# Attention probabilities turned in 32 by 32 blocks on VectorE and put together by DMA, in a gated cross-attention block

## The chip, the cores and the metric

The kernel runs on one core of a Trainium2 chip. A core has TensorE (matrix products, here also transposes), VectorE, ScalarE, GpSimd and SyncE (SP), which issues DMAs in the order of its own list; sixteen DMA engines move the data. The metric is the device time in microseconds (us), median of several runs. The engines run their own instruction lists and wait for each other by semaphores.

## The reference

The block adds gated cross-attention to `x`, and then a gated, quantized feed-forward network:

```python
# x (4, 512, 1024), ctx (4, 64, 1024); 32 heads of 128, 8 KV heads (each serves 4 heads)
def xattn(q, k, v, Wq, Wk, Wv, Wd):
    queries = rope(heads(q @ Wq.T)); keys = rope(heads(k @ Wk.T)); values = heads(v @ Wv.T)
    scores = einsum('bhqd,bhkd->bhqk', queries, repeat(keys, 4)) * 128 ** -0.5
    scores = where(causal, scores, lowest)
    attn = softmax(scores, axis=-1)                 # 512 queries x 64 keys per head
    return einsum('bhqk,bhkd->bhqd', attn, repeat(values, 4)) -> rows @ Wd.T

x = x + tanh(g_xattn[0]) * xattn(layernorm(x), ctx, ctx, Wq, Wk, Wv, Wd)
x = x + tanh(g_ffn[0]) * ffn(layernorm(x), ...)     # int8-like weights and rounded activations
```

## The kernel before

The four batch elements are done in two halves of two. In each half there are 32 *units*; a unit is a pair of heads with one batch element of the half (512 queries, 64 keys, two heads: 8 blocks of 64 columns, `prob`, 128 partitions x 512). Four units, two pairs of heads by two batch elements, make a *group*, which shares one KV head. Each engine has a hand-written list, `slot(half, u)`, by the kind of the slot, `u % 4`; kind 0 begins a group. Slot u computes the queries of unit u (eight steps `queries(unit, part)`, each of two times three matmuls, since every float32 product is made of a high and a low half), the scores of unit u - 1, and the turning of the probabilities of unit u - 2, and it carries the sixteen output steps of the group before (`outputs(gg - 1, c)`, six matmuls each, 3, 5, 5 and 3 of them in kinds 0 to 3). Eight values steps (`values(gg, i)`, three matmuls: values times a piece of the output weights) are spread over kinds 2, 3 and the next 0. Outputs steps 0 to 7 read the turned probabilities of the group's units 0 and 2, steps 8 to 15 those of units 1 and 3. `last_outputs` does the rest of the last group of a half.

The way of a unit's probabilities: VectorE does the mask, maximum and subtraction (`softmax_a`), ScalarE the exponential, VectorE the sum, the reciprocal and the product (`softmax_b`). TensorE then turns four blocks of 128 x 128 into a PSUM bank (`turn_probs`, line 544), ScalarE copies them rounded to `pt_hi` (line 837), VectorE subtracts to get `pt_lo` (`lower_probs`, line 1112 by `lower`), and the output steps read both. ScalarE's copy waits until the output steps of the group before have read the buffer (`o_ps`).

The lists are in order, so an instruction that waits holds back all behind it. In kind 3 ScalarE's list is: split weights 8g+3, copy values 2, split 8g+4, split a query weight, copy values 3, split 8g+5, `copy_probs`, split a query weight, split 8g+6, exponential, copy values 4 and 5. VectorE's: `turn_second` (rotation), adds 13 to 15 with values 2 and 3 lowered between them, `lower_probs`, `softmax_a`, `turn_first`, values 4, `softmax_b`, values 5. The first queries step of a slot waits for the `turn_first` of the unit before. An output step c waits until VectorE has added step c - 2 (two PSUM banks).

SP issues the loads: query weights `wq_raw` (four DMAs for each pair of heads), output weights `wd_raw` (a ring of three, `WDS`; load v + 3 is issued by `next_wd(v)` once values step v has run, line 341), keys `kblk`, values `v_t`. Its list waits too.

Of the kernel before, what the change touches and what calls it, by code (L numbers as in the profile page):

```python
# [91 lines left out]
def gated_block(nc, x, ctx_t, g_att, g_ffn, wq_t, wk_t, wv_t, wd_t, wg_t, wu_t, wo_t,  # L92
# [6 lines left out]
    with root:  # L99
# [3 lines left out]
        def sb(stack, name, shape, dt):  # L103
            return stack.enter_context(nc.sbuf_tensor(name, [P] + shape, dt))
# [32 lines left out]
        with ExitStack() as s:  # L137
            pt_hi = sb(s, "pt_hi", [2, HB, CH], F32R)
            pt_lo = sb(s, "pt_lo", [2, HB, CH], F32R)
# [20 lines left out]
            acc = sb(s, "acc", [HTILES, DIM], F32)  # L160

# [56 lines left out]
        pt_ps, pt_hi_done, pt_lo_done = sem("pt_ps"), sem("pt_hi_done"), sem("pt_lo_done")  # L218
# [19 lines left out]
        Q_BANK, S_BANK, T_BANK, O_BANK, V_BANK = 0, 2, 3, 4, 6  # L238
        scores, p_turned = bank(S_BANK), bank(T_BANK)
# [34 lines left out]
        def _(sp):  # L274
# [83 lines left out]

            load_k(0)
            load_v(0)  # L360
            for half in range(HALVES):
                for u in range(UNITS):
                    unit, gg = half * UNITS + u, half * GROUPS + u // UPG
                    if u % 2 == 0 and unit // 2 + 1 < HALVES * PAIRS and unit != UNITS:
                        if unit >= 2:
                            sp.wait_ge(q_done, unit)
                        load_wq(unit // 2 + 1)
# [13 lines left out]
                    if u % UPG == 3:  # L381
                        for i in range(2, 6):
                            next_wd(VPG * gg + i)
                    if u == 3 and half == 1:
                        for t in range(HTILES):
                            sp.wait_ge(x1_store[t], 16)
                            sp.wait_ge(part_done, TILES + t + 1)
                            sp.dma_start(acc[:, t, :], x[HTILES + t, :, :]).then_inc(x_in[t], 16)
                if half == 0:
# [11 lines left out]
                    load_v(GROUPS)  # L401
                    sp.wait_ge(xt_ps, HTILES + 1)
# [6 lines left out]
            sp.wait_ge(q_done, HALVES * UNITS)  # L409

# [41 lines left out]
        def _(pe):  # L452
# [86 lines left out]
            def turn_probs(unit):  # L539
                pe.wait_ge(p_done, unit + 1)  # L540
                if unit:
                    pe.wait_ge(pt_lo_done, unit)
                for t in range(BT):
                    ins = pe.transpose(p_turned[:, t * P:(t + 1) * P], prob[:, 2 * t:2 * t + 2, :].rearrange("p a b -> p (a b)"), ident)  # L544
                ins.then_inc(pt_ps, 1)

# [28 lines left out]
            def slot(half, u):  # L575
                unit, gg, kind, filled = half * UNITS + u, half * GROUPS + u // UPG, u % UPG, u >= UPG
                queries(unit, 0)
                if kind == 0:
                    if filled:
                        turn_probs(unit - 2)  # L580
# [26 lines left out]
                if kind == 1:  # L607
                    if filled:
                        turn_probs(unit - 2)
                        outputs(gg - 1, 3)  # L610
# [16 lines left out]
                if kind == 2:  # L627
                    turn_probs(unit - 2)
# [20 lines left out]
                if kind == 3:  # L649
# [10 lines left out]
                    turn_probs(unit - 2)  # L660
# [9 lines left out]
            def last_outputs(half):  # L670
                unit, gg = (half + 1) * UNITS, (half + 1) * GROUPS
                turn_probs(unit - 2)
# [10 lines left out]
                turn_probs(unit - 1)  # L683
# [86 lines left out]
        def _(act):  # L770
# [61 lines left out]
            def copy_probs(unit):  # L832
                p, b, gg = (unit // HB) % 2, unit % HB, unit // UPG
                act.wait_ge(pt_ps, unit + 1)
                if gg >= 1:
                    act.wait_ge(o_ps, (gg - 1) * OPG + (b + 1) * 2 * BT)
                act.activation(pt_hi[:, p, b, :], p_turned, ACT.Copy).then_inc(pt_hi_done, 1)  # L837
# [270 lines left out]
        def _(dve):  # L1108
# [122 lines left out]
            def softmax_a(unit):  # L1231
# [9 lines left out]
                if unit:  # L1241
                    dve.wait_ge(pt_ps, unit)
# [3 lines left out]
            def softmax_b(unit):  # L1246
# [8 lines left out]
                                  ALU.mult).then_inc(p_done, 1)  # L1255

            def lower_probs(unit):
                p, b = (unit // HB) % 2, unit % HB
                dve.wait_ge(pt_hi_done, unit + 1)
                lower(pt_lo[:, p, b, :], p_turned, pt_hi[:, p, b, :], pt_lo_done)  # L1260
# [268 lines left out]
```

## Time and profile before

| | |
|---|---|
| median of 3 runs | 1,588.74 us (1,587.85 to 1,589.26) |
| the profiled execution | 1,585.7 us, its span 1,583.9 us |
| granted TensorE clock, mean | 0.983 |
| busy: TensorE, VectorE, ScalarE, GpSimd | 94%, 63%, 34%, 38% |
| DMA queue q1 | 197,536 packets, 138.67 MB, 30.8% of 16 engines' span |

A row of the costliest groups reads: line, engine, operation, output <- inputs, count | busy us, mean ns of one | idle of the engine just before them and what ended it. Timeline rows start with the start and the duration in us; matmuls overlap, so the distance between two starts is what one costs. A row on SPq gives the time for which an issue held SP.

### The profile page before, as it was taken

What the parts mean: (1) busy time and instruction counts of PE and PEld (TensorE: products, weight loads), DVE (VectorE), ACT (ScalarE), POOL (GpSimd) and SP (SyncE); (2) the same over time, 40 slices, a digit from 0 to 9 for tenths busy, and PEclk for the clock granted to TensorE, in tenths of its full rate; (3) what the DMA queues carried; (4) which work ended last, traced back from release to release, by engine and by line L of the source; (5) the groups of instructions that cost most, each with busy time, mean ns of one, the idle gap of its engine ahead of it and who ended that gap; (6) DMA issues with size and microseconds to landing.
All of it is one profiled execution on the core that took longest, in us unless ns stands there. A gap on an engine that the chain in (4) does not pass through costs nothing.

```text
span 1583.9 us, 19344 instructions
## 1 busy us (share of the span) xinstructions
PE 1490.7 (94%) x7507; PEld 1223.5 (77%) x7520; DVE 993.9 (63%) x1562; ACT 539.1 (34%) x832; POOL 603.8 (38%) x392
## 2 busy tenths in 40 slices
PE   6879999999999999998898999999999999976996
PEld 5858888888888888886777888888888888854553
DVE  5747565656565656666474656565656565668995
ACT  3323232323232323244242313232323232317884
POOL 0044333343434333330333333333333434214996
PEclk9999999999999999999999999999999999998999
DMA  8723222221222222227233222222222211192553
GB/s 268 229 49 84 65 61 68 58 68 57 68 56 69 60 65 62 65 61 242 52 146 75 64 52 60 53 59 55 58 55 56 55 56 46 37 282 85 195 178 141
DMA packets 198058, 143.05 MB, mean 90 GB/s; under 512 B 147152, under 2 KB 167760, under 8 KB 197584
## 3 DMA queue, kind: packets, MB, share of 16 engines
q1 hardware_dynamic: 197536, 138.67, 30.8%
q0 software_dynamic: 432, 3.15, 0.9%
q8 instruction: 60, 0.98, 0.3%
q14 instruction: 30, 0.25, 0.1%
HBM read 125.01 MB, written 19.92 MB: 92 GB/s over the span
## 4 chain that ended last, share of the span: by engine, by line
PE 80%; DVE 8%; ACT 4%; POOL 3%; issue 2%; DMA 1%; SPq 1%; POOLq 0%; DVEq 0%; ACTq 0%
PE psum L455 16%; PE psum L457 16%; PE psum L456 16%; PE psum L535 7%; PE psum L570 7%; PE psum L572 7%; PE psum L571 7%; POOL go L1084 2%; PE psum L544 2%; DVE stat L1150 1%; DVE sc L1422 1%; ACT xg L973 1%; DMA kv_w<-in_wk_t 1%; ACT xu L974 1%; PE psum L502 1%
## 5 line engine op out<-in xcount | busy, mean ns | idle before, releaser
L455 PE MATMUL psum<-xt_hi,wq_hi 128*128 128x512 f32 x1024 | 407.0, 397 | 13.3 <-DVE rot L1220 8.6
L457 PE MATMUL psum<-xt_hi,wq_lo 128*128 128x512 f32 x1024 | 401.0, 392 | 0.0
L456 PE MATMUL psum<-xt_lo,wq_hi 128*128 128x512 f32 x1024 | 400.6, 391 | 0.0
L1028 POOL TENSOR_TENSOR rot<-rot 128x1024 f32<-128x1024 f32 x64 | 153.4, 2397 | 467.7 <-DVE rot L1228 465.8
L1276 DVE TENSOR_TENSOR acc<-psum,acc 128x512 f32<-128x512 f32 x256 | 175.7, 688 | 164.2 <-PE psum L572 162.1
L1007 POOL TENSOR_TENSOR wd_lo<-wd_raw,wd_hi 128x512 fp32r<-128x512 f32 x128 | 164.1, 1288 | 227.6 <-ACT wd_hi L795 227.6
L1007 POOL TENSOR_TENSOR wq_lo<-wq_raw,wq_hi 128x512 fp32r<-128x512 f32 x128 | 162.7, 1286 | 202.6 <-ACT wq_hi L790 202.6
L455 PEld LDWEIGHTS psum<-xt_hi,wq_hi 128*128 128x128 f32 x1024 | 193.6, 189 | 53.1 <-issue 5.2
L1112 DVE TENSOR_TENSOR vw_lo<-psum,vw_hi 64x512 fp32r<-64x512 f32 x256 | 176.2, 689 | 81.1 <-ACT vw_hi L848 75.3
L457 PEld LDWEIGHTS psum<-xt_hi,wq_lo 128*128 128x128 f32 x1024 | 193.4, 189 | 41.2
L456 PEld LDWEIGHTS psum<-xt_lo,wq_hi 128*128 128x128 f32 x1024 | 193.9, 189 | 38.6
L848 ACT ACTIVATE vw_hi<-psum 64x512 fp32r<-64x512 f32 x256 | 151.3, 591 | 210.3 <-PE psum L457 207.2
L570 PE MATMUL psum<-vw_hi,pt_hi 128*128 128x512 f32 x512 | 206.7, 404 | 6.5 <-DVE pt_lo L1112 4.3
L572 PE MATMUL psum<-vw_hi,pt_lo 128*128 128x512 f32 x512 | 200.5, 392 | 0.0
L571 PE MATMUL psum<-vw_lo,pt_hi 128*128 128x512 f32 x512 | 200.4, 391 | 0.0
L837 ACT ACTIVATE pt_hi<-psum 128x512 fp32r<-128x512 f32 x64 | 38.3, 598 | 303.0 <-PE psum L544 303.0
L852 ACT ACTIVATE prob<-prob 128x512 f32<-128x512 f32 x64 | 40.3, 630 | 285.1 <-DVE prob L1243 285.1
L535 PEld LDWEIGHTS psum<-kblk,rot 128*128 128x128 f32 x1024 | 126.6, 195 | 10.3 <-issue 5.2
L1235 DVE TENSOR_TENSOR psum<-psum,cst 128x128 f32<-128x128 f32 x64 | 19.2, 299 | 180.6 <-PE psum L535 180.6
L535 PE MATMUL psum<-kblk,rot 128*128 128x128 f32 x1024 | 127.2, 278 | 4.4 <-POOL rot L1028 4.4
L570 PEld LDWEIGHTS psum<-vw_hi,pt_hi 128*128 128x128 f32 x512 | 96.9, 189 | 28.1 <-DVE pt_lo L1112 5.7
L572 PEld LDWEIGHTS psum<-vw_hi,pt_lo 128*128 128x128 f32 x512 | 96.5, 189 | 20.7
(118 smaller groups left out, 1961.1 us busy)
## 6 DMA issues: line engine op xcount, KB each, us to landing
wq_raw<-in_wq_t SPq DMA_DIRECT2D x128, 256.0 KB, 4.5
wd_raw<-in_wd_t SPq DMA_DIRECT2D x128, 256.0 KB, 3.0
acc<-in_x SPq DMA_DIRECT2D x16, 512.0 KB, 8.1
x_scratch<-acc SPq DMA_DIRECT2D x16, 512.0 KB, 7.4
xa<-x_scratch SPq DMA_DIRECT2D x16, 512.0 KB, 3.3
xb<-x_scratch SPq DMA_DIRECT2D x16, 512.0 KB, 4.3
xn<-in_x SPq DMA_DIRECT2D x10, 512.0 KB, 4.3
kv_w<-in_wk_t SPq DMA_DIRECT2D x4, 1024.0 KB, 8.5
```

The lines of the kernel that those rows point to most:

```text
L455: pe.matmul(dst, a_hi, b_hi, start=start, stop=False)
L456: pe.matmul(dst, a_hi, b_lo, start=False, stop=False)
L457: return pe.matmul(dst, a_lo, b_hi, start=False, stop=stop)
L535: ins = pe.matmul(scores[:, t * P:(t + 1) * P], rot[:, 0, j, t * P:(t + 1) * P], kblk[:, j, 2 * b:2 * b + 2, :].rearrange("p a k -> p (a k ...
L570: pe.matmul(dst, p_hi, vw_hi[:, p, b, cols], start=(p == 0), stop=False)
L571: pe.matmul(dst, p_hi, vw_lo[:, p, b, cols], start=False, stop=False)
L572: ins = pe.matmul(dst, p_lo, vw_hi[:, p, b, cols], start=False, stop=(p == 1))
L848: act.activation(vw_hi[rows, p, bl, cols], bank(V_BANK + i % 2)[rows, :], ACT.Copy).then_inc(vw_hi_done, 1)
L1007: pool.tensor_tensor(dst, full, hi.bitcast(F32), ALU.subtract).then_inc(done, 1)
L1028: pool.tensor_tensor(rot[:, 0, :, :], rot[:, 0, :, :], rot[:, 1, :, :], ALU.add).then_inc(rope_done, 1)
L1112: dve.tensor_tensor(dst, full, hi.bitcast(F32), ALU.subtract).then_inc(done, 1)
L1276: dve.tensor_tensor(acc[:, tile, cols], bank(O_BANK + c % 2), acc[:, tile, cols], ALU.add).then_inc(o_done, 1)
```

## The change

`turn_probs` is gone from TensorE's list, and its PSUM bank is unused. At the end of `softmax_b` VectorE turns `prob` in 32 by 32 blocks into a new buffer `turned`. SP then puts each block in its place with sixteen DMAs of 32 partitions x 4 x 32 elements (`move_probs`), from quadrant a to quadrant c, into `pt_raw`, which shares its memory with `pt_lo`. ScalarE rounds `pt_raw` to `pt_hi` and VectorE lowers `pt_raw` in place. The wait for the output steps of the group before moves from ScalarE to SP.

```diff
         with ExitStack() as s:
             pt_hi = sb(s, "pt_hi", [2, HB, CH], F32R)
+            with ExitStack() as over:
+                pt_raw = sb(over, "pt_raw", [2, HB, CH], F32)
             pt_lo = sb(s, "pt_lo", [2, HB, CH], F32R)
...
+            turned = sb(s, "turned", [BT, 4, 32], F32)
...
+            def move_probs(unit):
+                p, b, gg = (unit // HB) % 2, unit % HB, unit // UPG
+                if gg >= 1:
+                    sp.wait_ge(o_ps, (gg - 1) * OPG + (b + 1) * 2 * BT)
+                sp.wait_ge(turned_done, unit + 1)
+                dst = pt_raw[:, p, b, :].rearrange("q (t a i) -> q t a i", a=4, i=32)
+                for a in range(4):
+                    for c in range(4):
+                        sp.dma_start(dst[32 * c:32 * c + 32, :, a, :], turned[32 * a:32 * a + 32, :, c, :]).then_inc(pt_in[unit % 2], 16)
...
                     unit, gg = half * UNITS + u, half * GROUPS + u // UPG
+                    if u % UPG == 3:
+                        move_probs(unit - 2)
                     if u % 2 == 0 and unit // 2 + 1 < HALVES * PAIRS and unit != UNITS:
...
                         for i in range(2, 6):
                             next_wd(VPG * gg + i)
+                    if u % UPG != 2 and u >= 1:
+                        move_probs(unit - 1)
...
+                    move_probs(UNITS - 1)
...
+            move_probs(HALVES * UNITS - 1)
...
-            def turn_probs(unit):
-                pe.wait_ge(p_done, unit + 1)
-                if unit:
-                    pe.wait_ge(pt_lo_done, unit)
-                for t in range(BT):
-                    ins = pe.transpose(p_turned[:, t * P:(t + 1) * P], prob[:, 2 * t:2 * t + 2, :].rearrange("p a b -> p (a b)"), ident)
-                ins.then_inc(pt_ps, 1)
...
             def copy_probs(unit):
-                p, b, gg = (unit // HB) % 2, unit % HB, unit // UPG
-                act.wait_ge(pt_ps, unit + 1)
-                if gg >= 1:
-                    act.wait_ge(o_ps, (gg - 1) * OPG + (b + 1) * 2 * BT)
-                act.activation(pt_hi[:, p, b, :], p_turned, ACT.Copy).then_inc(pt_hi_done, 1)
+                p, b = (unit // HB) % 2, unit % HB
+                act.wait_ge(pt_in[unit % 2], 256 * (unit // 2 + 1))
+                act.activation(pt_hi[:, p, b, :], pt_raw[:, p, b, :], ACT.Copy).then_inc(pt_hi_done, 1)
...
-                if unit:
-                    dve.wait_ge(pt_ps, unit)
...
                                   ALU.mult).then_inc(p_done, 1)
+                dve.wait_ge(p_done, unit + 1)
+                if unit:
+                    dve.wait_ge(pt_in[(unit - 1) % 2], 256 * ((unit - 1) // 2 + 1))
+                dve.transpose(turned[:, :, :, :], prob[:, :, :].rearrange("p (t h) (m k) -> p t (h m) k", t=BT, k=32)).then_inc(turned_done, 1)
...
-                lower(pt_lo[:, p, b, :], p_turned, pt_hi[:, p, b, :], pt_lo_done)
+                lower(pt_lo[:, p, b, :], pt_raw[:, p, b, :], pt_hi[:, p, b, :], pt_lo_done)
```

SP's list from kind 2 of one group to the key load in kind 0 of the next, before the change; a row is a DMA, what it waits for and how many alike follow:

```order
L300 DMA wq_raw<-in_wq_t 128x8x64 [waits q_done]
L300 DMA wq_raw<-in_wq_t 128x8x64 x3
L306 DMA wd_raw<-in_wd_t 128x512 [waits vw_ps] x6
L300 DMA wq_raw<-in_wq_t 128x8x64 [waits q_done]
L300 DMA wq_raw<-in_wq_t 128x8x64 x3
L306 DMA wd_raw<-in_wd_t 128x512 [waits vw_ps]
L336 DMA kblk<-kv_scratch 64x2x64 [waits s_done]
```

The same place after it, with the move that kind 1 leaves ahead of it:

```order
L372 DMA pt_raw<-turned 32x4x32 [waits turned_done,o_ps]
L372 DMA pt_raw<-turned 32x4x32 x15
L304 DMA wq_raw<-in_wq_t 128x8x64 [waits q_done]
L304 DMA wq_raw<-in_wq_t 128x8x64 x3
L310 DMA wd_raw<-in_wd_t 128x512 [waits vw_ps] x2
L372 DMA pt_raw<-turned 32x4x32 [waits turned_done,o_ps]
L372 DMA pt_raw<-turned 32x4x32 x15
L310 DMA wd_raw<-in_wd_t 128x512 [waits vw_ps] x4
L372 DMA pt_raw<-turned 32x4x32 [waits turned_done,o_ps]
L372 DMA pt_raw<-turned 32x4x32 x15
L304 DMA wq_raw<-in_wq_t 128x8x64 [waits q_done]
L304 DMA wq_raw<-in_wq_t 128x8x64 x3
```

The six loads of output weights in a row are now two and four, with a move between them, and each query weight load stands behind a move.

VectorE's list in kind 3, from the lower half of the probabilities to values 5, before:

```order
L1112 TENSOR_TENSOR pt_lo<-psum,pt_hi 128x512 [waits pt_hi_done]
L1235 TENSOR_TENSOR psum<-psum,cst 128x128 [waits s_done]
L1239 TENSOR_REDUCE red<-psum 128x8 [waits mask_done]
L1243 TENSOR_TENSOR prob<-psum,red 128x512 [waits pt_ps,max_done]
L1220 TENSOR_TENSOR rot<-psum,cst 128x1024 [waits s_done,qa_done]
L1112 TENSOR_TENSOR vw_lo<-psum,vw_hi 64x512 [waits vw_hi_done] x2
L1248 TENSOR_REDUCE red<-prob 128x8 [waits exp_done]
L1250 RECIPROCAL red<-red 128x8 [waits sum_done]
L1252 TENSOR_SCALAR red<-red,gates 128x8 [waits rcp_done]
L1254 TENSOR_TENSOR prob<-prob,red 128x512 [waits share_done]
L1112 TENSOR_TENSOR vw_lo<-psum,vw_hi 64x512 [waits vw_hi_done] x2
```

And after:

```order
L1116 TENSOR_TENSOR pt_lo<-pt_raw,pt_hi 128x512 [waits pt_hi_done]
L1239 TENSOR_TENSOR psum<-psum,cst 128x128 [waits s_done]
L1243 TENSOR_REDUCE red<-psum 128x8 [waits mask_done]
L1245 TENSOR_TENSOR prob<-psum,red 128x512 [waits max_done]
L1224 TENSOR_TENSOR rot<-psum,cst 128x1024 [waits s_done,qa_done]
L1116 TENSOR_TENSOR vw_lo<-psum,vw_hi 64x512 [waits vw_hi_done] x2
L1250 TENSOR_REDUCE red<-prob 128x8 [waits exp_done]
L1252 RECIPROCAL red<-red 128x8 [waits sum_done]
L1254 TENSOR_SCALAR red<-red,gates 128x8 [waits rcp_done]
L1256 TENSOR_TENSOR prob<-prob,red 128x512 [waits share_done]
L1261 STREAM_TRANSPOSE turned<-prob 128x512 [waits pt_in1,p_done]
L1116 TENSOR_TENSOR vw_lo<-psum,vw_hi 64x512 [waits vw_hi_done] x2
```

One instruction is added behind the product, with a wait for the moves of the unit before; the subtraction no longer waits for TensorE's turn.

## Rows read from the trace of the kernel before

**Rows 1.** The page's busy times: us, share of the span, instructions.

```profile
PE 1490.7 (94%) x7507; PEld 1223.5 (77%) x7520; DVE 993.9 (63%) x1562; ACT 539.1 (34%) x832; POOL 603.8 (38%) x392
```

**Rows 2.** The page's chain that ended last, by engine.

```profile
PE 80%; DVE 8%; ACT 4%; POOL 3%; issue 2%; DMA 1%; SPq 1%; POOLq 0%; DVEq 0%; ACTq 0%
```

**Rows 3.** Windows, one steady group: length, busy per engine, clock, DMA share, GB/s.

```profile
401.32:481.17 79.85, 79.85 (x393) 67.28 (x392) 48.51 (x74) 22.43 (x40) 29.80 (x20) 1.00 0.26 64
```

**Rows 4.** Timeline of TensorE in kind 3, from the slot's first queries step.

```profile
373.39 0.39 PE L455 MATMUL psum<-xt_hi,wq_hi 128*128 128x512 f32 x1
...
374.75 0.39 PE L570 MATMUL psum<-vw_hi,pt_hi 128*128 128x512 f32 x1
...
376.11 0.39 PE L455 MATMUL psum<-wd_hi,v_t 128*128 128x512 f32 x1
...
382.91 0.60 PE L544 MATMUL psum<-cst,prob 128*128 128x128 f32 x4
...
384.05 0.39 PE L455 MATMUL psum<-xt_hi,wq_hi 128*128 128x512 f32 x1
...
384.75 1.95 PE L535 MATMUL psum<-kblk,rot 128*128 128x128 f32 x16
386.45 0.48 PE L455 MATMUL psum<-xt_hi,wq_hi 128*128 128x512 f32 x1
...
391.30 0.39 PE L455 MATMUL psum<-wd_hi,v_t 128*128 128x512 f32 x1
```

**Rows 5.** Timeline of VectorE in the same slot: mask, rotation, sum, product.

```profile
386.73 0.30 DVE L1235 TENSOR_TENSOR psum<-psum,cst 128x128 f32<-128x128 f32 x1 [1.86 <-PE psum L535]
...
388.40 1.21 DVE L1220 TENSOR_TENSOR rot<-psum,cst 128x1024 f32<-128x1024 f32 x1
...
391.10 0.69 DVE L1248 TENSOR_REDUCE red<-prob 128x8 f32<-128x512 f32 x1
...
392.32 0.69 DVE L1254 TENSOR_TENSOR prob<-prob,red 128x512 f32<-128x512 f32 x1
```

**Rows 6.** The page's costliest groups: output weights lowered, values copied, probabilities copied.

```profile
L1007 POOL TENSOR_TENSOR wd_lo<-wd_raw,wd_hi 128x512 fp32r<-128x512 f32 x128 | 164.1, 1288 | 227.6 <-ACT wd_hi L795 227.6
...
L848 ACT ACTIVATE vw_hi<-psum 64x512 fp32r<-64x512 f32 x256 | 151.3, 591 | 210.3 <-PE psum L457 207.2
...
L837 ACT ACTIVATE pt_hi<-psum 128x512 fp32r<-128x512 f32 x64 | 38.3, 598 | 303.0 <-PE psum L544 303.0
```

**Rows 7.** Three lines' DMA issues: SP held (ns min/median/max), us from issue to landing.

```profile
L336 SPq DMA_DIRECT2D kblk<-kv_scratch x64: 584/606/1343, 78.9 to 1316.2; - x64
...
DMA to landing us min/median/max: 2.0/2.2/4.3
...
L306 SPq DMA_DIRECT2D wd_raw<-in_wd_t x128: 327/333/1717, 58.5 to 1379.6; - x128
...
DMA to landing us min/median/max: 2.9/3.0/5.6
...
L300 SPq DMA_DIRECT2D wq_raw<-in_wq_t x128: 545/674/8558, 49.7 to 1306.7; - x128
```

**Rows 8.** Timeline of SP's queue: four issues in a row, twice.

```profile
393.54 3.15 SPq L300 DMA_DIRECT2D wq_raw<-in_wq_t  x4
...
403.29 2.55 SPq L336 DMA_DIRECT2D kblk<-kv_scratch  x4
```

**Rows 9.** Windows and timeline of TensorE after an idle at the half's end.

```profile
720.00:722.00 2.00, 1.51 (x4) 1.22 (x5) 0.00 (x0) 0.00 (x0) 0.44 (x1) 0.50 0.76 217
...
720.49 0.80 PE L455 MATMUL psum<-wd_hi,v_t 128*128 128x512 f32 x1 [3.12 <-POOL wd_lo L1007]
...
723.22 0.46 PE L570 MATMUL psum<-vw_hi,pt_hi 128*128 128x512 f32 x1
```

**Rows 10.** Timeline of TensorE in the last outputs of half 1: steps 0 and 8.

```profile
1386.16 0.51 PE L570 MATMUL psum<-vw_hi,pt_hi 128*128 128x512 f32 x1 [0.71 <-DVE pt_lo L1112]
...
1407.98 0.50 PE L570 MATMUL psum<-vw_hi,pt_hi 128*128 128x512 f32 x1 [1.41 <-DVE pt_lo L1112]
```

More of the change, by code:

```diff
@@ L217, in gated_block @@
         sum_done, rcp_done, share_done, p_done = sem("sum_done"), sem("rcp_done"), sem("share_done"), sem("p_done")
-        pt_ps, pt_hi_done, pt_lo_done = sem("pt_ps"), sem("pt_hi_done"), sem("pt_lo_done")
+        turned_done, pt_hi_done, pt_lo_done = sem("turned_done"), sem("pt_hi_done"), sem("pt_lo_done")
+        pt_in = [sem("pt_in0"), sem("pt_in1")]
         vw_ps, vw_hi_done, vw_lo_done = sem("vw_ps"), sem("vw_hi_done"), sem("vw_lo_done")
@@ L235, in gated_block @@
         out_store = [sem(f"out_store{k}") for k in range(4)]
-        Q_BANK, S_BANK, T_BANK, O_BANK, V_BANK = 0, 2, 3, 4, 6
-        scores, p_turned = bank(S_BANK), bank(T_BANK)
+        Q_BANK, S_BANK, O_BANK, V_BANK = 0, 2, 4, 6
+        scores = bank(S_BANK)
         def turn_banks(half, t):
@@ L578, in slot @@
                 if kind == 0:
-                    if filled:
-                        turn_probs(unit - 2)
                     queries(unit, 1)
@@ L608, in slot @@
                     if filled:
-                        turn_probs(unit - 2)
                         outputs(gg - 1, 3)
@@ L627, in slot @@
                 if kind == 2:
-                    turn_probs(unit - 2)
                     if filled:
@@ L659, in slot @@
                         outputs(gg - 1, 15)
-                    turn_probs(unit - 2)
                     queries(unit, 3)
@@ L671, in last_outputs @@
                 unit, gg = (half + 1) * UNITS, (half + 1) * GROUPS
-                turn_probs(unit - 2)
                 values(gg - 1, 6)
@@ L682, in last_outputs @@
                     outputs(gg - 1, c)
-                turn_probs(unit - 1)
                 if half == 0:
```

## The prediction

> **What bounds the kernel now.** I read the page first, for which engine is busy; then the chain of waits; then one steady group by windows; then the timelines of TensorE, VectorE and SP for one slot. TensorE is busy 94% of the span and VectorE 63% [rows 1], and the chain that ended last lies 80% on TensorE [rows 2]. In a steady group (four slots, one KV head) TensorE is busy all 79.85 us and VectorE 48.5 [rows 3]. So for most of the span TensorE's list of matmuls is the time: whatever leaves it is won, and whatever makes it wait is lost. Against that stands a queue which nobody waits for today: SP, which issues the DMAs.
>
> One step (6 matmuls) of queries or outputs takes 1.36 us of TensorE, a values step, three matmuls, half of that, a score 1.8 (1.70 and a slower first matmul behind it) [rows 4]. With 8 query steps in each slot, 3, 5, 5 and 3 output steps in kinds 0 to 3, 2, 0, 2 and 4 values steps and one score, the slots take 18.1, 19.5, 20.8 and 19.5 us: 78.0 us, and four turns make 79.85.
>
> **What leaves.** Four transposes per unit: from 382.91 to 384.05 the turn and three matmuls take 1.14 us, where three matmuls take 0.68 [rows 4], so a turn costs 0.46 us; 64 of them are 29.5 us. This is the whole gain on TensorE.
>
> **What comes, per unit.** VectorE turns 128x512 values in blocks. No such instruction is in the trace; its other passes over 128x512 take 0.69 us [rows 5], a ScalarE pass 0.60 [rows 6]; one over twice the columns 1.21 [rows 5], which I take as the slow end, and 0.60 as the fast one. I take 0.7, the row over the same tile. It also moves the release of the move behind the probabilities. VectorE has 31 us idle per group, so its busy time costs nothing; its place in the chain below does. ScalarE's copy (0.6) and VectorE's lower half (0.7) stay, now out of SBUF; nothing speaks for another duration.
>
> Sixteen DMAs on SP, each 32 partitions x 4 runs of 128 bytes. SBUF to SBUF is not in the trace. Bounds of one issue: the 128x512 weight loads wd_raw hold SP 0.33 us, the kblk loads 0.61 (four take 2.55, so one each 0.64), the wq_raw loads 0.67 (four in 3.15, one each 0.79) [rows 7, 8]. The kblk load is nearest: also a part of the partitions, and 128 short runs or fewer. I take 0.64: 16 hold SP for 10.2 us. The last lands 2.2 us after its issue (kblk; wd_raw 3.0), so **a move takes 15 x 0.64 + 2.2 = 11.8 us** from its release. It can't come out below 2.2, the landing of a single one.
>
> The Trainium skill (DMA: Bandwidth & Descriptors, section Anatomy of one DMA) puts the sequencer's dispatch at about 50 ns and nearly all of a DMA's fixed 2 us in the receipt. By that sixteen would land 3 us after release, and the sum would come to some 1,610 us. The landing agrees with rows 7; the 0.33 to 0.79 us for which one issue holds SP do not, and the measurement decides.
>
> **Where it lies on the path.** Times from the start of a kind 3 slot of group g (373.39 in the trace), with no turns.
> Kind 3: the move of unit 4g+1 overwrites what outputs step 15 reads, so it waits for it: 9.5. Issues run to 19.7, the last lands at 21.3. Behind them in SP's queue is the load of weights 8g+5 (lands 3.0 later, 22.8), which until now was issued before step 15. ScalarE splits it (0.6), GpSimd lowers it (1.3 [rows 6]): 24.8. TensorE wants it for values step 5 at 17.4 (391.30 less 373.39 and a turn): **7.4 us of waiting**. ScalarE's copy of the probabilities stands behind that split (24.0), VectorE's lower half ends at 24.7, and behind it stand the first part of the softmax (1.85 with its gaps: from 386.73 to just past the rotation's start at 388.40 [rows 5]), and the rotation (1.2), which releases the next slot's queries: 27.8, another 1.0. Exponential (0.6), values copy (two of 0.6 [rows 6]), values lower (two of 0.7), second part of the softmax (1.95 from 391.10 [rows 5]) and the new turn then end at about 32.1.
> Kind 0 (starts 27.8): the move of unit 4g+2 lands at 43.9, copy and lower end at 45.4. Outputs step 0 wants it after 4.8 us of slot, at 32.6: **12.8 us**. Its score ends at 50.1, the turned probabilities of 4g+3 are there at 57.4 (behind a values lower of 1.4 and the rotation).
> Kind 1 (58.9): that move lands at 69.2; copy, lower and output add 3 end at 71.4, outputs step 5 wants the bank at 68.9: **2.5 us**.
> Kind 2 (81.0): the move of 4g+4 waits for outputs step 7 and its turn, 78.6; lands 90.4; copy, lower and add 8 end at 92.6; outputs step 10 wants that at 87.8: **4.8 us**. The slot ends at 106.7.
> So a group takes 106.7 us and not 79.85: **+26.8**, the turns' gain counted in.
>
> The clock: after 3.1 us of idle, from 720.49 to 723.22 a matmul took 0.6 us or more and the granted clock was 0.50, the 1.2 GHz level [rows 9]; six matmuls in 2.73 us instead of 1.36, so some 1.3 us lost. At the end of the second half an idle of 1.4 us before 1408 was followed by full speed [rows 10]. Of the four waits, the one of kind 3 is covered by that of kind 0; kind 0 would pay 2 and kind 2 1: +3 per group.
>
> **The sum**, against the profiled run (1,585.7 us, span 1,583.9): 14 full groups x (26.8 + 3) = 417. The two ends of a half: from the last slot's end to outputs step 8 took 22 us (from step 0 at 1386.2 to step 8 at 1408.0 [rows 10]); now, from the last slot's end at 27.8, step 0 waits to 45.4 as above, the score ends at 50.8, its probabilities are turned 5.4 later, and with 11.8 + 1.4 step 8 starts at 69.5: 42 us instead of 22, and 2 for the clock, 44 for both halves. The first group of a half has no outputs, but VectorE stands behind the copies: 7.5 each, 15. 1,585.7 + 417 + 44 + 15 = 2,062. The median shown is 3 us above this run: **about 2,062 us stays my number**, the 3 being less than any rounding here.
>
> **Bounds.** With 0.36 us per issue a move takes 7.6 us and holds SP 5.8: waits of 3 + 1, 8.6, 0 and 0.7 per group, 11.4 net, with a clock share of 1.5: 14 x 12.9 = 181, ends 22, first groups 10: 1,799. With 0.79: 14.05 us, each of the four stages 2.3 longer: 14 x 9.2 + 10 more, 2,200. A block turn of 1.21 adds 0.5 at three places a group, 21 us. Bytes: 131,072 more packets; the trace's average is 0.308 x 16 x 1,583.9 / 197,536 = 40 ns of one engine, so 128 packets per engine in a move are 5 us, under the 10.2 of issuing.
>
> **Rivals.**
> 1. *The same waits, cheap issues* (0.33 to 0.45): 1,800 to 1,890. For it: wd_raw's rows. Against: the only load that takes part of the partitions has 0.61.
> 2. *Dear moves*: issues as wq_raw's or packets of twice the average, so that the rings bind: 2,150 to 2,250. For it: one wq_raw issue held SP 8.6 us [rows 7], behind a full queue.
> 3. *Nearly free issues* (under 0.1). A move then takes 3 us. Weights 8g+5 land at 13.4 of kind 3, in time; VectorE's softmax starts 2.4 late behind the copies, the turned probabilities are there at 22.7, the move, copy and lower end at 27.1, and outputs step 0 wants them at 24.3: 2.8 us of waiting against 1.9 of gain, 14 x 0.9 and some 12 at the ends, 1,610. Against: the shortest issue in rows 7 is 0.33. The Trainium skill's dispatch figure, named above, would end here.
> 4. *Faster*: the moves hide and only the turns' gain stays, 1,585.7 - 29.5 = 1,556. The softmax's end (393.0) lies 19.6 us into kind 3, outputs step 0 at 19.95 + 4.8 + 0.5 = 25.2 [rows 4, 5]: 5.6 us; less the block turn 0.7 and copy and lower 1.4, 3.5 are left for a move. With a landing of 2.2 the other fifteen issues may take 1.3 us, under 0.09 each: it turns there, and only if kind 3 doesn't slip as in rival 3.
>
> **Chances.** My forecast, issues near 0.6 (1,930 to 2,150): 0.62, time 2,062; rival 1 0.17; rival 2 0.16; rival 3 0.02; rival 4 0.02; 0.01 for a sum of gain and waits that comes to nothing. Faster and slower count from 0.2%, about what a measurement of this kernel can tell: faster 0.02, same 0.01, slower 0.97. The range takes rivals 1 and 2 nearly whole: 1,800 to 2,210.
>
> **What the next profile would show.** Right: the move's DMA issues near 0.6 us each, 1,024 of them; ScalarE's pt_hi waiting for those DMAs in every slot; TensorE idle before outputs step 0 (some 13 us) and before values step 5 (some 7); a group near 107 to 110 us; the granted clock well under 1.00 at the middle of the span. Wrong: TensorE still busy through a steady group, or its waits ending on VectorE's passes with the DMAs long landed. If the issues take 0.6 and the group is not near 107, the path above is wrong; if they don't, only their size.

## The result, and the profile after

| | before | after |
|---|---|---|
| median | 1,588.3 us (1,585.66 to 1,589.26, 4 runs) | 2,119.85 us (2,119.3 to 2,125.37, 4 runs) |
| span of the profiled execution | 1,583.9 us | 2,118.2 us |
| granted TensorE clock, mean | 0.983 | 0.866 |
| a steady group (eleven, from outputs step 0 to outputs step 0) | 79.85 us | 110.1 to 114.5, mean 112.9; the one shown 113.4 |

The changed kernel takes 1.336 times as long (95% interval 1.334 to 1.3382). Forecast were 2,062 us and a range of 1,800 to 2,210: the time is 58 us above the number and inside the range. Two executions further down, one of experiment 4 (2,659 us) and one of the kernel before beside experiments 1 to 4 (2,183 us), ran at a lower clock throughout and are in no number.

The page of the changed kernel: busy times, the granted clock in 40 slices, the chain that ended last by engine; it answers to [rows 1, 2].

```profile
PE 1599.8 (76%) x7264; PEld 1282.8 (61%) x7264; DVE 1040.7 (49%) x1626; ACT 537.0 (25%) x832; POOL 609.0 (29%) x392
...
PEclk9788979798988889796988889897979897977899
...
PE 37%; SPq 29%; DVE 13%; DMA 9%; ACT 6%; issue 5%; POOL 2%; POOLq 0%; ACTq 0%; DVEq 0%
```

TensorE has 243 instructions fewer and is busy 109 us longer; it idles 518 us instead of 93. The chain, which before lay 80% on TensorE and 1% on SP's queue, now lies 29% on SP's queue and 9% on DMAs. A "busy" matmul may be a slow one: this row alone says that the clock has a part in the loss.

The costliest groups that answer to [rows 6], each with the idle time of its engine before it:

```profile
L583 PE MATMUL psum<-vw_hi,pt_hi 128*128 128x512 f32 x512 | 227.7, 445 | 292.0 <-DVE pt_lo L1116 201.3
...
L1116 DVE TENSOR_TENSOR pt_lo<-pt_raw,pt_hi 128x512 fp32r<-128x512 f32 x64 | 54.7, 855 | 664.5 <-ACT pt_hi L841 664.5
...
L841 ACT ACTIVATE pt_hi<-pt_raw 128x512 fp32r<-128x512 f32 x64 | 40.0, 625 | 741.8 <-DMA pt_raw<-turned 741.8
...
L801 ACT ACTIVATE wd_hi<-wd_raw 128x512 fp32r<-128x512 f32 x128 | 78.1, 621 | 247.1 <-DMA wd_raw<-in_wd_t 246.4
```

Read from the DMA on, that is a chain: ScalarE waits 741.8 us for moves, VectorE 664.5 us for ScalarE's copies, TensorE 201.3 us for VectorE's lower halves. The last row is the second way: ScalarE also waits 246.4 us for output weights, loads that stand behind a move in SP's list.

The steps of one move, by line (count, then min/median/max in ns):

```profile
L372 SPq DMA_DIRECT2D pt_raw<-turned x1024: 585/601/1555, 125.4 to 1937.4; - x171
...
DMA to landing us min/median/max: 1.8/1.9/6.4
...
L1261 DVE STREAM_TRANSPOSE turned<-prob x64: 711/711/716, 124.6 to 1926.5; 128x512 f32<-128x512 f32 x64
```

The block turn is 0.71 us, an issue holds SP 0.60 us, and its DMA lands 1.9 us after the issue began: forecast were 0.7, 0.64 with its spacing, and 2.2.

The timeline of SP and of the three engines behind it, in a kind 3 slot of the changed kernel and up to outputs step 0 of the next (start, duration, row, idle before and who ended it):

```profile
600.80 11.05 SPq L372 DMA_DIRECT2D pt_raw<-turned  x16
...
611.90 1.54 SPq L310 DMA_DIRECT2D wd_raw<-in_wd_t  x3
...
616.21 0.63 ACT L801 ACTIVATE wd_hi<-wd_raw 128x512 fp32r<-128x512 f32 x1 [16.92 <-DMA wd_raw<-in_wd_t]
616.75 0.61 ACT L841 ACTIVATE pt_hi<-pt_raw 128x512 fp32r<-128x512 f32 x1
616.92 1.27 POOL L1011 TENSOR_TENSOR wd_lo<-wd_raw,wd_hi 128x512 fp32r<-128x512 f32 x1 [17.76 <-ACT wd_hi L801]
...
617.39 1.34 DVE L1116 TENSOR_TENSOR pt_lo<-pt_raw,pt_hi 128x512 fp32r<-128x512 f32 x1 [15.89 <-ACT pt_hi L841]
...
618.15 1.73 POOL L1011 TENSOR_TENSOR wq_lo<-wq_raw,wq_hi 128x512 fp32r<-128x512 f32 x1
...
618.25 0.80 PE L476 MATMUL psum<-wd_hi,v_t 128*128 128x512 f32 x1 [9.55 <-POOL wd_lo L1011]
...
624.97 0.71 DVE L1261 STREAM_TRANSPOSE turned<-prob 128x512 f32<-128x512 f32 x1
...
625.77 10.54 SPq L372 DMA_DIRECT2D pt_raw<-turned  x16
...
637.55 0.63 ACT L841 ACTIVATE pt_hi<-pt_raw 128x512 fp32r<-128x512 f32 x1 [14.29 <-DMA pt_raw<-turned]
...
638.22 0.69 DVE L1116 TENSOR_TENSOR pt_lo<-pt_raw,pt_hi 128x512 fp32r<-128x512 f32 x1 [9.97 <-ACT pt_hi L841]
...
638.96 0.79 PE L583 MATMUL psum<-vw_hi,pt_hi 128*128 128x512 f32 x1 [11.37 <-DVE pt_lo L1116]
```

The rows show the forecast's chain link by link. Sixteen issues hold SP from 600.80 to 611.85. The first weight load behind them starts at 611.90 and is there at 616.2. Split, lowered by GpSimd, it frees TensorE at 618.25 (values step 5, 9.55 us of idle). VectorE's softmax is late by then; its block turn ends at 625.7, the next move holds SP from 625.77 to 636.3 and lands at 637.5, and outputs step 0 starts at 638.96, after 11.37 us of idle.

Four windows, each the 5 us of TensorE from the end of one of the four waits of a steady group, and the group itself, which answers to [rows 3] (length, busy of each engine, clock, DMA share, GB/s):

```profile
575.36:580.36 5.00, 5.00 (x18) 4.14 (x19) 1.23 (x2) 0.11 (x1) 0.00 (x0) 0.66 0.66 130
618.25:623.25 5.00, 5.00 (x12) 3.95 (x13) 4.82 (x8) 2.92 (x6) 2.87 (x2) 0.51 0.16 52
638.96:643.96 5.00, 5.00 (x13) 3.94 (x14) 1.93 (x3) 1.54 (x4) 1.27 (x1) 0.54 1.06 211
666.51:671.51 5.00, 5.00 (x15) 3.95 (x16) 4.86 (x9) 1.34 (x3) 4.22 (x4) 0.66 0.01 4
561.85:675.27 113.42, 86.69 (x377) 71.10 (x376) 51.32 (x78) 22.85 (x40) 30.10 (x20) 0.86 0.25 54
```

The group of 113.42 us is 86.69 busy and 26.73 idle. The same work at full clock is 78.0 (experiment 1 shows 77.92). So 8.7 us a group is TensorE at a lower clock; the four windows hold 5 x (0.34 + 0.49 + 0.46 + 0.34) = 8.2 of it.

### The profile page after: what moved, and what is told of

The parts are those of the page before. It is cut to its first block, busy times and chain, and to the rows that moved or that the text cites. A ratio compares the mean times of both kernels' runs of the same rounds, so it can differ in the third digit from the quotient of the medians.

```text
span 2118.2 us, 19870 instructions
## 1 busy us (share of the span) xinstructions
PE 1599.8 (76%) x7264; PEld 1282.8 (61%) x7264; DVE 1040.7 (49%) x1626; ACT 537.0 (25%) x832; POOL 609.0 (29%) x392
## 4 chain that ended last, share of the span: by engine, by line
PE 37%; SPq 29%; DVE 13%; DMA 9%; ACT 6%; issue 5%; POOL 2%; POOLq 0%; ACTq 0%; DVEq 0%
SPq L372 28%; PE psum L476 6%; PE psum L477 6%; PE psum L478 6%; PE psum L583 5%; PE psum L585 4%; PE psum L584 4%; DMA pt_raw<-turned 4%; DMA wd_raw<-in_wd_t 3%; PE psum L556 3%; DVE pt_lo L1116 2%; ACT pt_hi L841 2%; POOL go L1088 1%; DVE vw_lo L1116 1%; DVE acc L1282 1%
## 5 line engine op out<-in xcount | busy, mean ns | idle before, releaser
L583 PE MATMUL psum<-vw_hi,pt_hi 128*128 128x512 f32 x512 | 227.7, 445 | 292.0 <-DVE pt_lo L1116 201.3
L476 PE MATMUL psum<-xt_hi,wq_hi 128*128 128x512 f32 x1024 | 430.3, 420 | 14.7 <-DVE rot L1224 11.0
L477 PE MATMUL psum<-xt_lo,wq_hi 128*128 128x512 f32 x1024 | 424.0, 414 | 0.0
L478 PE MATMUL psum<-xt_hi,wq_lo 128*128 128x512 f32 x1024 | 420.2, 410 | 0.0
L1116 DVE TENSOR_TENSOR pt_lo<-pt_raw,pt_hi 128x512 fp32r<-128x512 f32 x64 | 54.7, 855 | 664.5 <-ACT pt_hi L841 664.5
L841 ACT ACTIVATE pt_hi<-pt_raw 128x512 fp32r<-128x512 f32 x64 | 40.0, 625 | 741.8 <-DMA pt_raw<-turned 741.8
L584 PE MATMUL psum<-vw_lo,pt_hi 128*128 128x512 f32 x512 | 218.6, 427 | 0.0
L585 PE MATMUL psum<-vw_hi,pt_lo 128*128 128x512 f32 x512 | 217.9, 426 | 0.0
L476 PE MATMUL psum<-wd_hi,v_t 128*128 128x512 f32 x128 | 59.4, 464 | 147.1 <-POOL wd_lo L1011 134.5
L801 ACT ACTIVATE wd_hi<-wd_raw 128x512 fp32r<-128x512 f32 x128 | 78.1, 621 | 247.1 <-DMA wd_raw<-in_wd_t 246.4
```

Source lines behind the costliest of these rows:

```text
L476: pe.matmul(dst, a_hi, b_hi, start=start, stop=False)
L477: pe.matmul(dst, a_hi, b_lo, start=False, stop=False)
L478: return pe.matmul(dst, a_lo, b_hi, start=False, stop=stop)
L583: pe.matmul(dst, p_hi, vw_hi[:, p, b, cols], start=(p == 0), stop=False)
L584: pe.matmul(dst, p_hi, vw_lo[:, p, b, cols], start=False, stop=False)
L585: ins = pe.matmul(dst, p_lo, vw_hi[:, p, b, cols], start=False, stop=(p == 1))
```

## The experiments

The kernel before ran beside each of them; ratios are to it. The theory after the result: the loss is SP's queue, held 10 to 11 us by each move, through two things that stand behind it (the move's own landing, and the weight load 8g+5), and the clock after each wait. The first rival: the landing and the exchange of the blocks by DMA cost most, and the issues little. The second: VectorE's added pass and its new order cost.

### 1. No move at all

`move_probs` and its calls are gone; ScalarE and VectorE read `turned` itself, so the blocks are not exchanged between quadrants. The wait for the output steps of the group before is ScalarE's again.

```diff
-                for a in range(4):
-                    for c in range(4):
-                        sp.dma_start(dst[32 * c:32 * c + 32, :, a, :], turned[32 * a:32 * a + 32, :, c, :]).then_inc(pt_in[unit % 2], 16)
...
-                act.wait_ge(pt_in[unit % 2], 256 * (unit // 2 + 1))
-                act.activation(pt_hi[:, p, b, :], pt_raw[:, p, b, :], ACT.Copy).then_inc(pt_hi_done, 1)
...
+                act.wait_ge(turned_done, unit + 1)
+                if gg >= 1:
+                    act.wait_ge(o_ps, (gg - 1) * OPG + (b + 1) * 2 * BT)
+                act.activation(pt_hi[:, p, b, :], turned[:, :, :, :].rearrange("q t a i -> q (t a i)"), ACT.Copy).then_inc(pt_hi_done, 1)
...
-                lower(pt_lo[:, p, b, :], pt_raw[:, p, b, :], pt_hi[:, p, b, :], pt_lo_done)
+                lower(pt_lo[:, p, b, :], turned[:, :, :, :].rearrange("q t a i -> q (t a i)"), pt_hi[:, p, b, :], pt_lo_done)
```

> The changed kernel without its moves: ScalarE and VectorE read the block-turned buffer directly (left out: the sixteen DMAs per unit, so the blocks stay in their quadrants). Theory (all of the loss is in the moves): TensorE's gain of 64 x 0.46 us alone, 1,556 to 1,562 us, no idle of TensorE in a steady group. Rival (VectorE's added pass and the longer way of the probabilities cost of themselves): above 1,588, with TensorE waiting before outputs step 0.

Measured: 1,564.0 us (1,563.23 to 1,568.08), ratio 0.9868 (0.9849 to 0.9887). Two steady groups by windows:

```profile
161.98:239.90 77.92, 77.92 (x378) 65.70 (x378) 51.00 (x78) 23.20 (x42) 30.87 (x20) 1.00 0.26 66
239.90:317.82 77.92, 77.92 (x378) 65.71 (x378) 51.01 (x78) 22.73 (x41) 30.92 (x20) 1.00 0.26 65
```

TensorE never idles in a steady group, and VectorE has its 2.5 us more per group for nothing. The second rival falls. What leaves is worth 79.85 - 77.92 = 1.93 us a group, 31 for sixteen, near the 29.5 forecast; of it 23 us are seen, and the time is 2 us above the expected interval. By the two pages TensorE idles 98.9 us of the span here and 93.2 before: the difference of 5.7 lies outside the steady groups and is most of the missing rest. The whole loss of the changed kernel against this one, 556 us, comes with the moves.

### 2 and 3. The same move as one DMA, and as four

One DMA of 128 x 512 elements, then four of 32 x 512, each from a quadrant to itself. Bytes are the same, but blocks do not change quadrants.

```diff
-                for a in range(4):
-                    for c in range(4):
-                        sp.dma_start(dst[32 * c:32 * c + 32, :, a, :], turned[32 * a:32 * a + 32, :, c, :]).then_inc(pt_in[unit % 2], 16)
+                sp.dma_start(pt_raw[:, p, b, :], turned[:, :, :, :].rearrange("q t a i -> q (t a i)")).then_inc(pt_in[unit % 2], 16)
```

> One DMA of 128 partitions x 512 per unit in place of sixteen: the same bytes (left out: the crossing of the quadrants). Theory (the price is the number of issues, 0.64 us of SP each): a move takes 2 us, the path in kind 3 does not slip and outputs step 0 is met by a hair, 1,556 to 1,570 us. Rival (any DMA between VectorE's turn and the copy costs a wait, by landing and handoffs): 1,600 or more.

> Four DMAs of 32 partitions x 512 per unit, from each quadrant to itself: the same bytes in a quarter of the issues (left out: the crossing of the quadrants). Theory (number of issues): a move takes 3 x 0.64 + 1.9 = 3.8 us and holds SP 2.6; waits of 1.6 in kind 3 and 4.8 in kind 0, less 1.9 of gain, with the clock about 5.8 per group, 14 groups and the ends: 1,670 to 1,690 us. Rival (bytes or packets bind): close to 2,118, or as the one-DMA version with no difference between the two.

Measured: with one DMA 1,670.67 us, ratio 1.0542 (1.0516 to 1.0569), a group 83.1 to 86.2 us; with four 1,709.54 us, ratio 1.0779 (1.0762 to 1.0796), a group 85.0 to 88.9 us. With 4 issues a group instead of 64, 449 us leave the changed kernel. Both runs also leave out the crossing of the quadrants and move runs of 2 KB where the sixteen have 128 bytes. But the small DMAs land no later (1.9 us after their issue, the one of 256 KB 2.4), and in the changed kernel fifteen issues of 0.60 us make most of a move's length. So the number of issues is the main cost. Between 4 and 16 issues, one more per unit is worth (2,119.85 - 1,709.54) / 12 = 34 us, 2.1 us a group. The first rival falls in the main, but not whole: both runs came out slower than expected, by 101 and 20 us, and the one with one DMA lies where its rival had it, above 1,600. A DMA that lands 2.4 us after its release should nearly have been hidden. Its timeline shows why it isn't:

```profile
481.43 0.50 SPq L370 DMA_DIRECT2D pt_raw<-turned  x1
...
485.77 0.63 ACT L799 ACTIVATE wd_hi<-wd_raw 128x512 fp32r<-128x512 f32 x1 [5.84 <-DMA wd_raw<-in_wd_t]
486.31 0.62 ACT L839 ACTIVATE pt_hi<-pt_raw 128x512 fp32r<-128x512 f32 x1
486.48 1.29 POOL L1009 TENSOR_TENSOR wd_lo<-wd_raw,wd_hi 128x512 fp32r<-128x512 f32 x1 [6.66 <-ACT wd_hi L799]
486.95 1.36 DVE L1114 TENSOR_TENSOR pt_lo<-pt_raw,pt_hi 128x512 fp32r<-128x512 f32 x1 [4.83 <-ACT pt_hi L839]
...
497.91 2.34 POOL L1030 TENSOR_TENSOR rot<-rot 128x1024 f32<-128x1024 f32 x1 [7.19 <-DVE rot L1230]
498.43 2.37 DVE L1114 TENSOR_TENSOR pt_lo<-pt_raw,pt_hi 128x512 fp32r<-128x512 f32 x1 [0.60 <-ACT pt_hi L839]
...
500.85 0.80 PE L581 MATMUL psum<-vw_hi,pt_hi 128*128 128x512 f32 x1 [4.64 <-DVE pt_lo L1114]
```

Two things. The move waits in SP's list until the outputs of the group before have read the buffer, the load behind it with it, and ScalarE's copy of the probabilities, which landed at 484.96, stands behind the split of that load at 485.77: all of VectorE's softmax slips. The block turn of unit 4g+2 ends 1.0 us before TensorE is ready for outputs step 0; in experiment 1 it is 4.3 us. And the lower half, 0.69 us before, takes 1.36 and 2.37 us while GpSimd runs. Four DMAs show the same two waits:

```profile
494.64 0.50 PE L475 MATMUL psum<-wd_hi,v_t 128*128 128x512 f32 x1 [2.05 <-POOL wd_lo L1010]
...
507.67 0.79 PE L582 MATMUL psum<-vw_hi,pt_hi 128*128 128x512 f32 x1 [4.32 <-DVE pt_lo L1115]
```

### 4. The changed kernel, with two weight loads ahead of the kind 3 move

```diff
-                    if u % UPG == 3:
-                        move_probs(unit - 2)
...
                     if u % UPG == 3:
-                        for i in range(2, 6):
-                            next_wd(VPG * gg + i)
+                        next_wd(VPG * gg + 2)
+                        next_wd(VPG * gg + 3)
+                        move_probs(unit - 2)
+                        next_wd(VPG * gg + 4)
+                        next_wd(VPG * gg + 5)
```

> The changed kernel with one edit in SP's list of kind 3: the output weight loads behind values steps 2 and 3 are issued ahead of the move of unit 4g+1. It takes away TensorE's wait before values step 5 (9.5 us a group in the changed kernel). Theory (that wait is covered: the same move also holds VectorE's softmax and the next slot's first queries): only 2 to 2.5 us a group come back, 2,080 to 2,095 us, and TensorE now waits some 6 us at the first queries step of kind 0. Rival (the waits add up): 14 x 9.5 less, about 1,985 us.

Measured: 2,066.19 us (2,063.3 to 2,067.98, 3 runs), ratio 1.3023 (1.3 to 1.3047), 54 us under the changed kernel. The wait before values step 5 took 8.4 to 10.1 us in each of 14 groups, 128 us; taking away what makes it returns 54. So more than half of it is covered, as this theory had it, and the rival (the waits add up) falls. That with the softmax earlier the move for outputs step 0 is still the late one, and that TensorE now waits at the first queries step of kind 0, is argued, not shown. The time is 14 us below the expected interval: 3.8 us a group come back, of which one spell of low clock less may be a part (2.45 us in the window above). That share is not shown either.

### 5. One DMA and the loads first

Both edits together.

> The one-DMA version (quadrants not crossed) with the two output weight loads of kind 3 issued ahead of the move. Theory (what the one-DMA version paid was its place in SP's list: the load issued behind the move landed 3.8 us later, ScalarE's split of it stands ahead of the copy, and the softmax slipped by 2.4; the rest is VectorE's lower half, 1.4 to 2.4 us where both inputs are in SBUF and GpSimd is busy): the slip goes, a wait of 1 to 2 us in kind 0 stays, 1,580 to 1,605 us. Rival (landing and handoffs alone make the 84 us above the unmoved version): no more than 10 us come back, 1,660.

Measured: 1,615.89 us, ratio 1.0189 (1.0174 to 1.0205), 55 us under experiment 2, a group 79.8 to 83.3 us. The loads' place in SP's list is worth as much with one DMA as with sixteen. The rival (no more than 10 us come back) falls. The expectation missed by 11 us, and what stays is 1.6 to 3.5 us of idle in each steady group and the two ends:

```profile
484.05 0.72 PE L582 MATMUL psum<-vw_hi,pt_hi 128*128 128x512 f32 x1 [2.52 <-DVE pt_lo L1115]
```

This is outputs step 0, behind the unit whose softmax ends last: even a move of one DMA does not fit between it and its reader. Rival 4 of the prediction had 3.5 us left there after block turn, copy and lower; a DMA that lands 2.4 us after its release and a lower half that takes up to 2.2 us longer fill more than that (2.38 us for the half, 1.7 more than alone, in the group of this row).

### 6. All sixteen DMAs, their readers as late as they may be

The order of ScalarE's copies and VectorE's lower halves becomes units 0, 2, 1, 3 of a group. Units 0 and 1 are copied a slot later, in kind 3 and at the end of kind 0; unit 3 is copied later within kind 1; units 1 and 3, which are read from outputs step 8 on, now stand behind an exponential. SP issues query weights and two output weights ahead of the moves. It does the whole computation.

```diff
+        def place(unit):
+
+            return UPG * (unit // UPG) + (0, 2, 1, 3)[unit % UPG] + 1
...
                     split_wd(VPG * gg + 5)
-                    copy_probs(unit - 2)
+                    copy_probs(unit - 3)
```

> All sixteen DMAs for all units, complete computation. Units 4g, 4g+1 and 4g+3 are copied and lowered later than in the changed kernel (kind 3, the end of kind 0 and the end of kind 1), still ahead of the output steps that read them; SP issues loads ahead of moves where it can. Only unit 4g+2 keeps its tight place. Theory (the loss is latency at four places, of which three have slack in the lists): the waits of kinds 1, 2 and 3 go, in kind 0 some 10 us stay, 1,740 to 1,800 us. Rival (SP's 41 us of issuing per group, or VectorE and GpSimd hindering each other, set the pace whatever the order): above 1,950.

Measured: 1,797.42 us (1,796.17 to 1,801.59), ratio 1.1332 (1.1316 to 1.1347): 322 us under the changed kernel with the same 1,024 DMAs. A steady group by windows, its only wait, and VectorE's block turn of unit 4g+2 ahead of it:

```profile
359.99:451.94 91.95, 80.44 (x378) 67.30 (x378) 51.62 (x78) 23.21 (x42) 30.27 (x21) 0.93 0.30 67
...
432.98 0.71 DVE L1269 STREAM_TRANSPOSE turned<-prob 128x512 f32<-128x512 f32 x1 [3.04 <-DMA pt_raw<-turned]
...
446.69 0.80 PE L590 MATMUL psum<-vw_hi,pt_hi 128*128 128x512 f32 x1 [11.51 <-DVE pt_lo L1124]
```

91.95 - 80.44 is that wait, 11.5 us, the same as the changed kernel has at this place (11.37). Three of the four waits were the order's. This one is the move of unit 4g+2, 13.0 us from the end of its block turn (433.69) to its reader, with 1.5 us of cover. Without moves the cover is 4.3 us (experiment 1). It is less here because the turn itself waits 3.04 us for the DMAs of unit 4g+1, now late, to leave the one buffer `turned`; it does so in every group, by 2.1 to 3.2 us. So a part of this wait is the buffer's; a second `turned` was not tried, and neither were issues from a second engine's queue. And with one wait the clock costs 80.44 - 77.92 = 2.5 us.

### 7 and 8. A version for this wait

In 7, unit 4g+2 of each group is turned by TensorE as before the change and the other 48 by blocks, in the order of experiment 6. In 8, the last unit of each half too: 18 on TensorE and 46 by blocks. Both do the whole computation. The first lines are experiment 8's, the last ones stand in experiment 7.

```diff
+        def on_pe(unit):
+
+            return unit % UPG == 2 or unit % UNITS == UNITS - 1
...
                 if kind == 0:
+                    if filled:
+                        turn_probs(unit - 2)
```

> As the late version, but unit 4g+2 is turned on TensorE as in the kernel before; the other 48 units go by VectorE and DMAs. Complete computation. Theory (a move costs nothing where the lists leave it 12 us and more): TensorE wins 48 turns; the version without moves showed 23 us for 64, so 17 us: 1,567 to 1,574 us, faster than both kernels. Rival (the added SP and VectorE work costs something even off the path): 1,585 or more.

> The hybrid with the last unit of each half turned on TensorE too (18 units on TensorE, 46 by VectorE and DMAs), complete computation. The hybrid's steady group took 78.41 us against 79.85, which is 14 x 1.44 = 20 us won, and its trace shows the loss at the ends of the halves: waits of 6.3 and 9.6 us before outputs step 8, with the slow clock behind them. Theory (those two moves, released in the last outputs with 5 output steps of cover, ate the gain): they go, 1,569 to 1,577 us. Rival (the loss at the ends is elsewhere, in the row loads and x rows that SP issues there): above 1,583.

Measured: experiment 7 took 1,592.33 us (5 runs), ratio 1.0037 (1.0024 to 1.0049), a miss of 18 us that lies where its rival had it, above 1,585; experiment 8 took 1,575.93 us (1,573.8 to 1,576.88, 5 runs) beside 1,586.32 of the kernel before, ratio 0.993 (0.9916 to 0.9943). In experiment 7 the groups are right, 78.4 us, and the two ends lose; its rows before outputs step 8 of the last group of each half:

```profile
737.06 0.79 PE L606 MATMUL psum<-vw_hi,pt_hi 128*128 128x512 f32 x1 [6.31 <-DVE pt_lo L1148]
...
1411.39 0.79 PE L606 MATMUL psum<-vw_hi,pt_hi 128*128 128x512 f32 x1 [9.56 <-DVE pt_lo L1148]
```

The same two places in experiment 8, and a steady group of it:

```profile
733.72 0.50 PE L612 MATMUL psum<-vw_hi,pt_hi 128*128 128x512 f32 x1 [0.54 <-DVE pt_lo L1155]
...
1399.42 0.50 PE L612 MATMUL psum<-vw_hi,pt_hi 128*128 128x512 f32 x1 [1.41 <-DVE pt_lo L1155]
...
321.40:399.80 78.40, 78.40 (x381) 66.09 (x381) 50.82 (x78) 22.96 (x41) 30.23 (x20) 1.00 0.34 74
```

The group is 78.40 us, 1.45 under [rows 3]; three units off TensorE at 0.46 are 1.38. Experiment 8 beats both kernels: the kernel before by 10.4 us, the changed one by 544. The fourteen groups alone would give 20 us. TensorE idles 99.5 us of the span instead of 93.2, and its first outputs step starts at 164.4 us instead of 159.0; what delays that start is open.

## Why the prediction was right, and what it mis-sized

The direction and the mechanism were right, and each was shown by a run of its own: no moves and the kernel is faster (1), fewer issues and most of the loss goes (2, 3), another order of queue and readers and more than half of it goes (6), the tight units back on TensorE and it is gone (7, 8).

**What leaves, 29.5 us.** Right: 1.93 us a group (experiment 1), of 1.84 forecast.

**The move, 11.8 us.** Right. Issues 0.60 us, sixteen hold SP 10.2 to 11.5 (median 10.3), landing 1.9: from 625.77 to the copy at 637.55 it takes 11.8. The kblk load was the right row to price an issue by. The prediction set against this the dispatch of about 50 ns that the Trainium skill gives (DMA: Bandwidth & Descriptors, section Anatomy of one DMA). That section describes DMAs issued from GpSimd, and these go out from SP: for them 0.60 us an issue decides.

**The waits of a group, 28.5 us.** Measured 26.7, by place:

| wait before | forecast | measured |
|---|---|---|
| values step 5 (kind 3) and the next queries | 7.4 + 1.0 | 9.55 |
| outputs step 0 (kind 0) | 12.8 | 11.37 |
| outputs step 5 (kind 1) | 2.5 | 1.78 |
| outputs step 10 (kind 2) | 4.8 | 4.02 |

No wait is at a place where none was forecast. In kind 3, the load right behind a move lands 4.1 us after its issue in the median, not 3.0 [rows 7], and here 4.3; the queries' 1.0 us hides in the longer wait. In the others a landing of 1.9 and not 2.2 us takes a little off.

**The clock, 3 us a group: this is the mis-sized term.** It cost 8.7. The step that failed reads "Of the four waits, the one of kind 3 is covered by that of kind 0; kind 0 would pay 2 and kind 2 1". They start TensorE again at 618.25 and 638.96, and it works 9.3 us between them, back at full speed for the second half. Both pay, 2.45 and 2.3 us by the windows, and the wait of 1.78 us, after which [rows 10] let me expect nothing, was followed by 1.7 us lost as well. With 8.7 in place of 3 and 26.7 in place of 28.5, this group is 3.8 us above the forecast. Added up over all fourteen, from outputs step 0 to outputs step 0, the groups are 473 us longer than before and not 417: 56 of the 58 us. The waits, priced 1.8 us a group too dear, hid 25 us of the clock's error; that is luck. The prediction named a group "not near 107" as a sign that its path was wrong: the group is 113.4, but its waits are where the path has them, and what it lacks is the clock. Experiment 6 has one wait and pays 2.5 us: here the price was about 2 us for each wait after which the clock was low.

**The ends and first groups, 59 us.** The span is 534.3 us longer; less the 473 of the groups, 61 are left. From outputs step 0 to step 8 of the last group, where [rows 10] has 21.8 us, it is now 29.3; the rows on TensorE in half 1:

```profile
1911.28 0.79 PE L583 MATMUL psum<-vw_hi,pt_hi 128*128 128x512 f32 x1 [14.33 <-DVE pt_lo L1116]
...
1940.62 0.80 PE L583 MATMUL psum<-vw_hi,pt_hi 128*128 128x512 f32 x1 [8.38 <-DVE pt_lo L1116]
```

**"Nothing speaks for another duration"** of the lower half, now with both inputs in SBUF. Wrong: 855 ns in the mean instead of 691, and 1.34 us in kind 3, in the chain. It is worth under 1 us a group here, behind moves of 11.8 us, but in experiment 2 more than half of these passes took about twice their time or more.

**My reasons failed more in the experiments than in the prediction.** The expectation of 1,556 to 1,570 us for one DMA took the landing for the whole path and forgot that ScalarE's list puts the copy behind the split of a load which SP holds back. The prediction had that step ("ScalarE's copy of the probabilities stands behind that split"); the expectation dropped it because the move had become short. Experiment 7 forgot the two ends, where the last unit's move is as late for outputs step 8.

**Rivals.** 1 (cheap issues) and 2 (dear moves) ended at 1,890 and from 2,150: neither reached. For rival 2 the prediction had one query weight issue that held SP 8.6 us "behind a full queue"; in the trace it begins at 824.36 with nine DMAs ahead that have not landed, seven of them of 512 KB, and is let go at 832.91, when six have. The moves met nothing like it: none of their issues held SP over 1.6 us. 3 and 4 needed issues under 0.1 us; the least was 0.585. The bare moves of experiment 2 show that even then 4 would not have held in this order of the lists.

## What to carry to other kernels

Price a transfer cut into pieces by how long its issues hold the queue, from a row of the same shape, and then list what else stands in that queue and in the lists of its readers; here 4 issues instead of 1 cost 39 us and 16 instead of 4 cost 410. Price the clock for each wait by itself, also for one that another wait covers. When a transfer is long, first put its readers as late, and the loads beside it as early, as they may be: that took the loss from 34% to 13%. And when one unit of several is still late for its reader, keep the old way for that one alone: with 18 units of 64 on TensorE the 13% became a gain of 0.7%.

## What the runs showed of the hardware

**VectorE beside GpSimd.** The lower half with both inputs in SBUF takes 0.69 us alone and up to 2.9 us when GpSimd works. In the changed kernel 16 of the 64 began while a pass of GpSimd ran, and exactly these took 1.34 to 1.37 us; the other 48 took 0.69. Before, with one input in PSUM, 44 of the 64 began while GpSimd ran, and all 64 lay between 0.673 and 0.693. All passes of this kind, by line, in the kernel before, in the changed one and in experiment 2:

```profile
L1112 DVE TENSOR_TENSOR pt_lo<-psum,pt_hi x64: 673/691/693, 126.0 to 1407.2; 128x512 fp32r<-128x512 f32 x64
```

```profile
L1116 DVE TENSOR_TENSOR pt_lo<-pt_raw,pt_hi x64: 691/693/1366, 137.7 to 1939.9; 128x512 fp32r<-128x512 f32 x64
```

```profile
L1114 DVE TENSOR_TENSOR pt_lo<-pt_raw,pt_hi x64: 675/1361/2875, 130.4 to 1496.5; 128x512 fp32r<-128x512 f32 x64
```

In the timeline of the changed kernel above, GpSimd's pass from 616.92 ends at 618.19, VectorE's from 617.39 at 618.73, which is 0.54 later, and GpSimd's next, from 618.15, takes 1.73 us, where the median of its kind is 1.28. Each looks as if it began when the other ended. The Trainium skill (SBUF — State Buffer, section Who interferes with whom) has a rule for it: a VectorE instruction with two SBUF inputs contends with a GpSimd instruction that reads SBUF, and the pair of ports which the two engines share is an exclusive lock. By this rule the pass at 617.39 would end at 618.19 + 0.69 = 618.88, and it ended at 618.73; in experiment 2 the one at 498.43 would end at 500.25 + 0.69 = 500.94, and it ended at 500.80. The trace agrees within 0.15 us, for all 16 slow passes of the changed kernel. This rule spoke against the change and the prediction did not weigh it.

**The clock after a wait.** After 9.55 and 11.37 us of idle the mean granted clock over the next 5 us is 0.51 and 0.54, near the 1.2 GHz level; after 4.02 and 1.78 us it is 0.66. In each case some 2 us are lost; the forecast's price for one was 1.3 us, from an idle of 3.12 us [rows 9]. The three longer waits are followed by the low clock in every group. The shortest is not: of nine such waits of 1.76 to 1.82 us in the whole trace, five were followed by it, 1.0 to 1.6 us after TensorE had started again, and four by full speed. Three of the groups with these four are the shortest, 110.1 to 111.1 us.

**A load behind a move.** The output weight loads landed 3.0 us after their issue in the median before and 3.8 in the changed kernel, with the same bytes; those issued right behind a move take 4.1. It is not the number or the size of the move's DMAs: right behind a move of one DMA (experiment 2) it is 4.1 too, behind four 4.0, and in experiment 6 4.1. In the kernel before, where there are no moves, the 16 loads that were issued with three query weight loads under way took 4.0. What delays them is open.
